# One of a pair's two shifted additions moved from VectorE to a second exponential and an accumulating DMA

## The chip, the cores and the metric

The kernel runs on one core of a Trainium2 chip. The metric is device microseconds of one execution; the kernel is timed in several executions and the median is quoted. A profiled execution gives the rows quoted below. Engines are named as the profile does: PE (TensorE matmul), PEld (its weight load), DVE (VectorE), ACT (ScalarE), POOL (GpSimd), SP (SyncE, which here only issues DMAs).

## What is computed

Two layers of the same "contextual attention" run one after the other over 4 images of 64 channels and 80x80 pixels, so the kernel works through 8 units (layer, image). Cut to what matters, one unit is:

```python
f = b[:, :, ::2, ::2]                       # 40 x 40 positions
w = patches_3x3(f); raw_w = patches_4x4(b, stride 2)
wn = w / max(norm(w), 1e-4)
yi = softmax(10 * (w @ wn.T) * mm, over l) * mm     # 1600 x 1600 scores
patches = yi.T @ raw_w                      # each position's 4x4 patch
out = overlap_add(patches, stride 2) / 4    # pasted back to 80 x 80
```

The overlap-add means that neighbouring scores meet: pasting a 4x4 patch at stride 2 is done here by adding to each score row its neighbour shifted by one position (and by one row of positions), and then multiplying by plain 2x2 blocks of the image.

## The kernel before

Scores lie in SBUF in `G`, 123 partitions (three strips of 41 positions) by 14 tiles. A unit is worked in 4 column chunks (`P_CHUNKS`, 492, 492, 492 and 246 columns) by 7 pairs of tiles: 28 slots a unit. While unit u is pasted, the scores of unit v = u+1 are made, and the features of w = u+2 are prepared. Each engine runs a hand-written program, `body(u, v, w)`, over the 28 slots; the order on each engine is fixed, and semaphores hold the engines together.

For one pair `i` of chunk `k` the softmax and paste steps are, with the slots by which they run ahead of the paste:

- `argument_pair` (DVE, 4 slots ahead, line L923): scales the scores of the pair's two tiles, `arg_tiles(i)` = tiles 2i-1 and 2i, and subtracts the log-sum row held in PSUM (`psB`).
- `softmax_pair` (ACT, 4 slots ahead, L690): one exponential per tile, in place in `G`. On ACT's queue it stands between `copy_scores(j, 0)` and `copy_scores(j, 1)` (L665), which copy or bring score blocks of v from PSUM.
- `shift_pair` (SP, 4 slots ahead, L307): per tile, two DMAs copy the exponentials one partition down and one column on into a buffer of `SH`. The two DMAs are the partition ranges `SHIFT_PARTS`, 112 rows and 10 rows. `SH` has 4 buffers, two pairs' worth.
- `add_shifted` (DVE, 2 slots ahead, L934): `G += SH`, once per tile.
- `sum_pair` (DVE, 1 slot ahead, L952, L953 and L956): adds the tile above and writes `Z`, the weights' moving operand. It waits for the first added tile of the pair that follows, so for the first of the two additions that stand just before it on DVE's queue; the second runs meanwhile.
- `paste_tile` (PE, L504): `Z` times the blocks `B` into `psO`.

Between these, for v, PE makes score blocks (`products`, L454) or takes them by symmetry from stored ones (`transposes`, L463), ACT copies them (L652, L665), DVE combines them (L863) and multiplies and takes the maximum (`score_pair`, L869, L874), and ACT makes the sums of exponentials (`score_sums`, L679). Near the end of a unit the log-sum rows are worked out (`lse_*`, on PE L389), in two parts. SP also lays out the features of the next unit, from `LOHI` into `HL`, `LH`, `H1` and `HV` (`lay_out_features`, L288), loads images (L255), stores results (`store_chunk`, L295) and fetches the strips' border (`shift_strip`, L318, into `SHJ`). GpSimd only runs `wrap` (L1062), a small copy per pair of chunk 0. In the last unit no scores are left to make: the 28 slots hold only argument, exponentials, shifts, sums and paste. Below, "the last unit" is that stretch, from about 1388 us on.

A wait for two semaphores is written as a wait, then `sem_inc` on a gate semaphore, which gives the first wait an instruction to sit on, then the second wait on the operation itself.

Of the kernel before, what the change touches and what calls it, by code (L numbers as in the profile page):

```python
# [5 lines left out]
F32 = mybir.dt.float32  # L6
F16 = mybir.dt.float16
ALU = mybir.AluOpType
ACT = mybir.ActivationFunctionType
# [5 lines left out]
STRIPS, TILES = 3, 14  # L15
PITCH = HALF + 1
TW = STRIPS * PITCH
# [3 lines left out]
GLEN = TW + TILES * TW + WRAP  # L21
PAIRS = TILES // 2
# [7 lines left out]
SLOTS = NK * PAIRS  # L30
NB = NK * TILES
SHIFT_PARTS = [(0, 112), (112, TW - 1)]
STRIP_PARTS = [(0, 80), (80, WRAP)]
BIG = 1.0e30
FREE = 2
SFREE = 4
LSE_FIRST = 4
EXP_AND_LN = 6

# [4 lines left out]
LEAD = 4  # L44
# [36 lines left out]
def contextual_attention(nc, x, mask0, mask1, ident, valid, out):  # L81
    mid = nc.dram_tensor("mid", (IMAGES, C, SIDE, SIDE), F32, kind="Internal").ap()

    with ExitStack() as ctx:
        def sb(name, shape, dt):
            return ctx.enter_context(nc.sbuf_tensor(name, shape, dt))
# [4 lines left out]
        def sem(name):  # L91
            return ctx.enter_context(nc.semaphore(name))

        G = sb("G", [TW, TILES * GLEN], F32)
# [9 lines left out]
        LOHI = sb("LOHI", [128, FLEN], F16)  # L104
        LS, HS = LOHI[0:64, :], LOHI[64:128, :]
        RB = sb("RB", [TW, TILES * TW], F32)
        SH = sb("SH", [TW, SFREE, 4 * TW], F32)
        SHJ = sb("SHJ", [TW, 4 * TW], F32)
        Z = sb("Z", [TW, 2 * FREE, 4 * TW], F32)
        S = sb("S", [TW, 2 * FREE, 4 * TW], F32)  # L110
# [8 lines left out]
        nb = sb("nb", [TW, UNITS * TILES], F32)  # L119
# [61 lines left out]
        act_gate = sem("act_gate")  # L181
        dve_gate = sem("dve_gate")
        pe_gate = sem("pe_gate")
        pool_gate = sem("pool_gate")
# [3 lines left out]
        lse_rows = sem("lse_rows")  # L188
        wrap_made = sem("wrap_made")
        arg_made = sem("arg_made")  # L190
        y_made = sem("y_made")
        sh_in = [sem(f"sh_in{i}") for i in range(SFREE)]
        shj_in = sem("shj_in")
        y1_made = sem("y1_made")
        z_made = sem("z_made")
# [16 lines left out]
        def p_cols(k, wrap=False):  # L212

            s0, n = P_CHUNKS[k]
            return (s0 + 1) * TW, n * TW + (WRAP if wrap and k == NK - 1 else 0)

        def arg_tiles(i):

            return [(2 * i + TILES - 1) % TILES, 2 * i]

        def place(u, v, s):

            unit = u if s < SLOTS else v
            return None if unit is None else (unit, s % SLOTS // PAIRS, s % PAIRS)
# [23 lines left out]
        def _(sp):  # L248
# [49 lines left out]
            def shift_pair(at):  # L298
                u, k, i = at
                c0, n = p_cols(k)  # L300
                for j, t in enumerate(arg_tiles(i)):
                    o = k * TILES + 2 * i + j
                    sp.wait_ge(y_made, u * NB + o + 1)
                    sp.wait_ge(y1_made, u * NB + o + 1)
                    for p0, p1 in SHIFT_PARTS:
                        g = t * GLEN + c0
                        sp.dma_start(SH[p0 + 1:p1 + 1, o % SFREE, 1:n], G[p0:p1, g:g + n - 1]).then_inc(sh_in[o % SFREE], 16)  # L307

            def shift_strip(at):

                u, k, i = at
                c0, n = p_cols(k, True)
                sp.wait_ge(y1_made, u * NB + k * TILES + 1 + SFREE)
                sp.sem_inc(sp_gate, 1)
                sp.wait_ge(z_made, u * SLOTS + k * PAIRS + 1)
                above = (TILES - 1) * GLEN + c0 - TW
                for p0, p1 in STRIP_PARTS:
                    sp.dma_start(SHJ[PITCH + p0:PITCH + p1, 0:n], G[p0:p1, above:above + n]).then_inc(shj_in, 16)  # L318

# [40 lines left out]
            for u in range(UNITS):  # L360
                v, w = (n if n < UNITS else None for n in (u + 1, u + 2))
# [217 lines left out]
        def _(act):  # L579
# [35 lines left out]
            def scale_rows(v, g):  # L615
                act.wait_ge(r_psum, v * 4 + g + 1)
                n = min(4, TILES - 4 * g) * TW
                act.activation(RB[:, 4 * g * TW:4 * g * TW + n], ROW_BANK[g][:, 0:n], ACT.Copy).then_inc(r_rows, 1)

# [63 lines left out]
            def softmax_pair(at):  # L683
                u, k, i = at
                c0, n = p_cols(k)
                for j, t in enumerate(arg_tiles(i)):
                    act.wait_ge(arg_made, u * NB + k * TILES + 2 * i + j + 1)
                    act.sem_inc(act_gate, 1)
                    y = G[:, t * GLEN + c0:t * GLEN + c0 + n]
                    act.activation(y, y, ACT.Exp, bias=nb[:, bass.ds(u * TILES + t, 1)]).then_inc(y_made, 1)  # L690

# [26 lines left out]
            def body(u, v, w):  # L718
                for s in BODY:
# [21 lines left out]
                    if at and not pairs:  # L741
                        softmax_pair(at)
# [4 lines left out]
                    if s == 24 and at:  # L747
                        softmax_pair(at)
# [38 lines left out]
        def _(dve):  # L787
# [7 lines left out]
            dve.sem_inc(z_made, 1)  # L795
            dve.sem_inc(y1_made, SFREE)

# [40 lines left out]
            def score_pair(v, j):  # L838
# [11 lines left out]
                for par, read in enumerate((even_read, odd_read)):  # L850
                    if shared:
# [6 lines left out]
                        if b0:  # L858
# [10 lines left out]
                    dve.tensor_tensor_reduce(S[:, slot + par, 0:n], (odd if par else even)[:, 0:n],  # L869
                                             RB[:, s0 * TW:s0 * TW + n], 1.0, 0.0,  # L870
                                             ALU.mult, ALU.max, mx[:, slot + par:slot + par + 1]).then_inc(max_made, 1)
# [55 lines left out]
            def add_shifted(at):  # L927
                u, k, i = at
                c0, n = p_cols(k)
                for j, t in enumerate(arg_tiles(i)):  # L930
                    o = k * TILES + 2 * i + j
                    dve.wait_ge(sh_in[o % SFREE], (u * (NB // SFREE) + o // SFREE + 1) * 16 * len(SHIFT_PARTS))
                    g = G[:, t * GLEN + c0:t * GLEN + c0 + n]
                    dve.tensor_tensor(g, g, SH[:, o % SFREE, 0:n], ALU.add).then_inc(y1_made, 1)  # L934

            def sum_pair(at, s):
                u, k, i = at
                c0, n = p_cols(k, True)
                slot = 2 * (s % 2)
                dve.wait_ge(y1_made, u * NB + k * TILES + min(2 * i + 3, TILES) + SFREE)  # L940
                dve.sem_inc(dve_gate, 1)
                if k == NK - 1 and i == 0:
                    dve.wait_ge(wrap_made, (u + 1) * PAIRS)
                    dve.sem_inc(dve_gate, 1)
                if i == 0:
                    dve.wait_ge(shj_in, (u * NK + k + 1) * 16 * len(STRIP_PARTS))
                    dve.sem_inc(dve_gate, 1)

                dve.wait_ge(z_used, u * SLOTS + k * PAIRS + i + 1)
                g = G[:, :].rearrange("p (t c) -> p t c", c=GLEN)  # L950
                if i == 0:
                    dve.tensor_tensor(Z[:, slot, 0:n], g[:, 0, c0:c0 + n], SHJ[:, 0:n], ALU.add)  # L952
                    dve.tensor_tensor(Z[:, slot + 1, 0:n], g[:, 1, c0:c0 + n], g[:, 0, c0 - TW:c0 - TW + n],  # L953
                                      ALU.add).then_inc(z_made, 1)
                else:
                    dve.tensor_tensor(Z[:, slot:slot + 2, 0:n], g[:, 2 * i:2 * i + 2, c0:c0 + n],  # L956
                                      g[:, 2 * i - 1:2 * i + 1, c0 - TW:c0 - TW + n], ALU.add).then_inc(z_made, 1)

            def body(u, v, w):
                for s in BODY:  # L960
# [6 lines left out]
                    if at_y:  # L967
                        add_shifted(at_y)
                    at_z = place(u, v, s + 1)
                    if at_z:  # L970
                        sum_pair(at_z, s + 1)
# [56 lines left out]
            for u in range(UNITS):  # L1028
                at = slice(u * TILES, (u + 1) * TILES)
# [15 lines left out]
        @block.gpsimd  # L1045
        def _(pool):
            pool.memset(XP[:, :, :], 0.0).then_inc(xp_cleared, 1)
            pool.memset(SQ[:, :], 0.0).then_inc(cleared, 1)
            pool.memset(LOHI[:, :].bitcast(F32), 0.0).then_inc(cleared, 1)
            pool.wait_ge(cleared, CLEARED)  # L1050
            pool.sem_inc(pool_gate, 1)

            def wrap(u, i):

                if i == 0 and not (isinstance(u, int) and u == 0):
                    pool.wait_ge(z_made, u * SLOTS + 1)
                    pool.sem_inc(pool_gate, 1)
                pool.wait_ge(y1_made, u * NB + 2 * i + 2 + SFREE)
                pool.sem_inc(pool_gate, 1)
                g = G[:, :].rearrange("p (t c) -> p t c", c=GLEN)  # L1060
                g = g[:, 0::TILES - 1, :] if i == 0 else g[:, 2 * i - 1:2 * i + 1, :]
                pool.tensor_copy(g[:, :, GLEN - WRAP:GLEN], g[:, :, TW + PITCH:2 * TW]).then_inc(wrap_made, 1)  # L1062

            def body(u, v):
                for s in BODY:
                    if s < 5 and u is not None:
                        wrap(u, s + 2)
                    if s >= SLOTS and v is not None:
                        wrap(v, 2 * (s - SLOTS))
                        wrap(v, 2 * (s - SLOTS) + 1)  # L1070

            body(None, 0)
            for u in range(UNITS - 1):
                body(u, u + 1)
            body(UNITS - 1, None)


# [20 lines left out]
```

## Time and profile before

| | |
|---|---|
| time, 3 executions | median 1500.39 us (1499.33 to 1503.53) |
| profiled execution, its own time | 1502.71 us |
| its span, first to last instruction | 1500.9 us |
| granted TensorE clock, mean | 0.982 |
| busy | PE 92%, PEld 60%, DVE 81%, ACT 57%, POOL 4% |
| DMA | 149.14 MB, 99 GB/s mean |

A group's row gives busy time, mean length and the idle time just ahead of it on its engine. A window's row gives what each engine was busy in that stretch. A wait's row names the waiting engine and line, what it waited for, total, times and longest. The chain of work that ended last is listed as start, length and what; "issue" is time with no visible releaser, and SPq or DVEq is an engine's queue of non-computing instructions. PE's matmuls are pipelined, and a row that merges several ends with the last one's tail.

### The profile page before, as it was taken

The page shows a single profiled execution, that of the slowest core. Times are in us where ns is not written, and L with a number is a line of the kernel's source. Part 1 is how long each engine was busy: PE and PEld are TensorE (multiplying, and loading weights), DVE is VectorE, ACT ScalarE, POOL GpSimd, SP SyncE. Part 2 cuts the span into 40 slices and gives each one's busy share as a digit, 9 for nine tenths or more (in the row PEclk, how much of TensorE's full clock was granted, in tenths as well). Part 3 has the DMA queues.
Part 4 walks back from the last instruction along what each step waited for, and adds up shares of the span by engine and source line. Part 5 has one row for each costly group of instructions (what it writes and reads, how often), then busy time and mean ns, then how long its engine had stood idle before and what let it go on. Part 6 is the DMA issues. An engine that isn't in the chain of part 4 may idle for free.

```text
span 1500.9 us, 24213 instructions
## 1 busy us (share of the span) xinstructions
PE 1377.1 (92%) x7190; PEld 897.6 (60%) x7190; DVE 1220.5 (81%) x2831; ACT 859.8 (57%) x2233; POOL 54.8 (4%) x63
## 2 busy tenths in 40 slices
PE   4987999989999899998999899998999989999886
PEld 4765665656556565566656576566665656557333
DVE  4668889788888888888898878978888888888984
ACT  2667546666458565584555755666645755457431
POOL 1001000010000100001000000001000010000100
PEclk9998999999999999999999999999999999999999
DMA  5305462254622754136631556215462254523442
GB/s 100 45 1 136 104 124 77 55 154 110 126 68 69 167 107 107 53 98 149 126 88 42 134 119 132 81 50 142 106 135 71 62 149 102 114 58 89 124 137 64
DMA packets 181621, 149.14 MB, mean 99 GB/s; under 512 B 119986, under 2 KB 177394, under 8 KB 181490
## 3 DMA queue, kind: packets, MB, share of 16 engines
q1 hardware_dynamic: 181170, 146.60, 41.1%
q10 hardware_dynamic: 320, 0.99, 0.3%
q8 instruction: 57, 0.93, 0.3%
q14 instruction: 74, 0.61, 0.1%
HBM read 19.76 MB, written 13.11 MB: 22 GB/s over the span
## 4 chain that ended last, share of the span: by engine, by line
PE 39%; DVE 23%; SPq 13%; ACT 9%; issue 8%; DMA 7%; DVEq 0%; POOL 0%; ACTq 0%; POOLq 0%
PE psO L504 18%; PE psG L454 17%; DVE G L923 5%; SPq L307 5%; DVE Z L956 4%; DVE G L863 4%; DVE S L869 3%; SPq L288 3%; DVE G L934 3%; PE psG L463 3%; ACT S L679 3%; DMA HV<-LOHI 3%; SPq L255 3%; DMA SH<-G 2%; ACT G L690 2%
## 5 line engine op out<-in xcount | busy, mean ns | idle before, releaser
L504 PE MATMUL psO<-Z,B 123*128 123x492 f32 (+1 forms) x1792 | 760.9, 553 | 31.3 <-DVE Z L956 19.4
L504 PEld LDWEIGHTS psO<-Z,B 123*128 123x128 f32 x1792 | 324.4, 194 | 260.4 <-issue 180.5
L454 PE MATMUL psG<-LH,HL 128*123 128x246 f16 (+2 forms) x2616 | 408.6, 286 | 24.6 <-DMA HV<-LOHI 19.0
L454 PEld LDWEIGHTS psG<-LH,HL 128*123 128x123 f16 x2616 | 278.0, 138 | 157.9 <-issue 104.5
L869 DVE CUSTOM_DVE_ANT_0 S<-G,RB 123x492 f32<-123x492 f32 (+1 forms) x448 | 268.7, 606 | 86.7 <-DVE G L863 52.1
L690 ACT ACTIVATE G<-G,nb 123x492 f32<-123x492 f32 (+1 forms) x448 | 270.5, 649 | 97.7 <-DVE G L923 97.2
L679 ACT ACTIVATE S<-S,nm 123x480 f32<-123x480 f32 (+3 forms) x560 | 306.9, 554 | 3.5 <-DVE nm L874 3.3
L934 DVE TENSOR_TENSOR G<-G,SH 123x492 f32<-123x492 f32 (+1 forms) x448 | 251.7, 600 | 45.1 <-DMA SH<-G 44.4
L923 DVE SCALAR_TENSOR_TENSOR G<-G,RA,psB 123x492 f32<-123x492 f32 (+1 forms) x448 | 274.8, 656 | 0.3 <-issue 0.3
L665 ACT ACTIVATE G<-psG 123x492 f32<-123x492 f32 (+3 forms) x256 | 120.4, 473 | 189.8 <-PE psG L454 108.3
L956 DVE TENSOR_TENSOR Z<-G 123x984 f32<-123x984 f32 (+1 forms) x192 | 209.1, 1090 | 0.0
L863 DVE TENSOR_TENSOR G<-G,psG 123x492 f32<-123x492 f32 (+2 forms) x272 | 134.1, 493 | 78.4 <-ACT G L665 44.3
L652 ACT ACTIVATE G<-psG 123x246 f32<-123x246 f32 (+1 forms) x136 | 64.2, 472 | 232.8 <-PE psG L454 232.4
L454 PE MATMUL psG<-H 128*123 128x123 f16 (+3 forms) x872 | 194.7, 285 | 0.0
L463 PEld LDWEIGHTS psG<-idn,G 123*123 123x123 f32 x672 | 98.3, 196 | 70.3 <-ACT G L665 23.8
L463 PE MATMUL psG<-idn,G 123*123 123x123 f32 x672 | 113.4, 290 | 24.6 <-ACT G L665 15.2
L454 PEld LDWEIGHTS psG<-H 128*123 128x123 f16 x872 | 103.2, 137 | 20.9
L454 PE MATMUL psG<-HL 128*123 128x492 f16 (+2 forms) x392 | 112.2, 286 | 0.0
L679 ACT ACTIVATION_READ_ACCUMULATOR S<-S,nm 123x1 f32 x560 | 108.1, 193 | 0.0
L1062 POOL COPY G<-G 123x164 f32<-123x164 f32 x56 | 49.9, 892 | 1353.1 <-DVE Z L956 989.6
L699 ACT ACTIVATE OSB<-psO 128x492 f32<-128x492 f32 (+1 forms) x64 | 33.2, 576 | 72.3 <-PE psO L504 72.2
L454 PE MATMUL psG<-HV 128*123 128x246 f16 (+2 forms) x240 | 68.1, 284 | 0.0
(84 smaller groups left out, 580.4 us busy)
## 6 DMA issues: line engine op xcount, KB each, us to landing
SH<-G SPq DMA_DIRECT2D x336, 214.8 KB
SH<-G SPq DMA_DIRECT2D x112, 107.2 KB
SH<-G SPq DMA_DIRECT2D x336, 19.2 KB
XP<-x SPq DMA_DIRECT2D x20, 280.0 KB, 6.2
XP<-mid SPq DMA_DIRECT2D x20, 280.0 KB, 5.7
mid<-OSB SPq DMA_DIRECT2D x52, 80.0 KB, 2.3
out<-OSB SPq DMA_DIRECT2D x52, 80.0 KB, 2.3
HL<-LOHI SPq DMA_DIRECT2D x16, 246.5 KB, 3.5
```

What stands on the lines that cost most here:

```text
L307: sp.dma_start(SH[p0 + 1:p1 + 1, o % SFREE, 1:n], G[p0:p1, g:g + n - 1]).then_inc(sh_in[o % SFREE], 16)
L454: last = pe.matmul(psG[0:TW, bank, b0 * TW:b1 * TW], st[:, p:p + TW], mv[:, lo:lo + n], start=i == 0, stop=i == len(terms) - 1)
L463: last = pe.transpose(psG[0:TW, par, i * TW:(i + 1) * TW], G[:, c:c + TW], idn[0:TW, 0:TW])
L504: last = pe.matmul(psO[:, b, 0:n], B[:, o:o + 128], Z[:, 2 * (s % 2) + j, 0:n], start=t == 0, stop=t == TILES - 1)
L665: act.activation(G[:, c:c + n], psG[0:TW, par, 0:n], ACT.Copy).then_inc(part if shared else read, 1)
L679: last = act.activation(y, y, ACT.Exp, bias=nm[:, k * TILES + t:k * TILES + t + 1], accum_out=sg[:, c:c + 1])
L690: act.activation(y, y, ACT.Exp, bias=nb[:, bass.ds(u * TILES + t, 1)]).then_inc(y_made, 1)
L863: dve.tensor_tensor((odd if par else even)[:, b0 * TW:n], rows[:, p0 * TW:p0 * TW + n - b0 * TW], psG[0:TW, par, b0 * TW:n], ALU.add).then ...
L869: dve.tensor_tensor_reduce(S[:, slot + par, 0:n], (odd if par else even)[:, 0:n], RB[:, s0 * TW:s0 * TW + n], 1.0, 0.0, ALU.mult, ALU.max, ...
L923: dve.scalar_tensor_tensor(out=g, in0=g, scalar=RA[:, bass.ds(u * TILES + t, 1)], in1=psB[0:TW, k % 2, 0:n], op0=ALU.mult, op1=ALU.subtrac ...
L934: dve.tensor_tensor(g, g, SH[:, o % SFREE, 0:n], ALU.add).then_inc(y1_made, 1)
L956: dve.tensor_tensor(Z[:, slot:slot + 2, 0:n], g[:, 2 * i:2 * i + 2, c0:c0 + n], g[:, 2 * i - 1:2 * i + 1, c0 - TW:c0 - TW + n], ALU.add).t ...
```

## The change

For each pair, only the first tile, 2i-1, still goes through `SH` and DVE's addition. For the second tile, 2i, ACT makes the exponential twice: first into a buffer of a new tile `Y`, then, after the first tile's exponential, in place in `G`. GpSimd then issues one DMA that reads `Y`, shifted by one partition and one column, and adds it to `G` (122 rows of up to 491 f32, `accum_op`). `SH` and `Y` have two buffers each, one per pair. `softmax_pair` waits before writing `Y` until the accumulating DMA of the pair two before has landed, and for both arguments of its own pair (`arg_made >= 2*o + 2`) ahead of its first exponential. `sum_pair` and `wrap` wait for their pair's accumulating DMA as well. `sum_pair` still waits for the first tile of the pair that follows, which is now the only addition of that pair. On GpSimd's queue the new `add_copy` stands ahead of `wrap` in each slot.

```diff
-SFREE = 4
+SFREE = 2
...
         SH = sb("SH", [TW, SFREE, 4 * TW], F32)
+        Y = sb("Y", [TW, SFREE, 4 * TW], F32)
...
+        def y1_done(u, k, i):
+
+            n = u * SLOTS + k * PAIRS + i
+            return y1_in[n % SFREE], (n // SFREE + 1) * 16
...
             def shift_pair(at):
                 u, k, i = at
                 c0, n = p_cols(k)
-                for j, t in enumerate(arg_tiles(i)):
-                    o = k * TILES + 2 * i + j
-                    sp.wait_ge(y_made, u * NB + o + 1)
-                    sp.wait_ge(y1_made, u * NB + o + 1)
-                    for p0, p1 in SHIFT_PARTS:
-                        g = t * GLEN + c0
-                        sp.dma_start(SH[p0 + 1:p1 + 1, o % SFREE, 1:n], G[p0:p1, g:g + n - 1]).then_inc(sh_in[o % SFREE], 16)
+                o = u * SLOTS + k * PAIRS + i
+                g = arg_tiles(i)[0] * GLEN + c0
+                sp.wait_ge(y_made, 2 * o + 1)
+                sp.wait_ge(y1_made, o + 1)
+                for p0, p1 in SHIFT_PARTS:
+                    sp.dma_start(SH[p0 + 1:p1 + 1, o % SFREE, 1:n], G[p0:p1, g:g + n - 1]).then_inc(sh_in[o % SFREE], 16)
...
             def softmax_pair(at):
                 u, k, i = at
                 c0, n = p_cols(k)
+                o = u * SLOTS + k * PAIRS + i
+                t = arg_tiles(i)[1]
+                if o >= SFREE:
+
+                    act.wait_ge(*y1_done(u, k, i - SFREE))
+                    act.sem_inc(act_gate, 1)
+                act.wait_ge(arg_made, 2 * o + 2)
+                act.activation(Y[:, o % SFREE, 0:n], G[:, t * GLEN + c0:t * GLEN + c0 + n], ACT.Exp,
+                               bias=nb[:, bass.ds(u * TILES + t, 1)]).then_inc(y_copied, 1)
                 for j, t in enumerate(arg_tiles(i)):
-                    act.wait_ge(arg_made, u * NB + k * TILES + 2 * i + j + 1)
-                    act.sem_inc(act_gate, 1)
+                    if j == 1:
+                        act.wait_ge(y_copied, o + 1)
                     y = G[:, t * GLEN + c0:t * GLEN + c0 + n]
                     act.activation(y, y, ACT.Exp, bias=nb[:, bass.ds(u * TILES + t, 1)]).then_inc(y_made, 1)
...
             def add_shifted(at):
                 u, k, i = at
                 c0, n = p_cols(k)
-                for j, t in enumerate(arg_tiles(i)):
-                    o = k * TILES + 2 * i + j
-                    dve.wait_ge(sh_in[o % SFREE], (u * (NB // SFREE) + o // SFREE + 1) * 16 * len(SHIFT_PARTS))
-                    g = G[:, t * GLEN + c0:t * GLEN + c0 + n]
-                    dve.tensor_tensor(g, g, SH[:, o % SFREE, 0:n], ALU.add).then_inc(y1_made, 1)
+                o = u * SLOTS + k * PAIRS + i
+                t = arg_tiles(i)[0]
+                dve.wait_ge(sh_in[o % SFREE], (o // SFREE + 1) * 16 * len(SHIFT_PARTS))
+                g = G[:, t * GLEN + c0:t * GLEN + c0 + n]
+                dve.tensor_tensor(g, g, SH[:, o % SFREE, 0:n], ALU.add).then_inc(y1_made, 1)

             def sum_pair(at, s):
...
-                dve.wait_ge(y1_made, u * NB + k * TILES + min(2 * i + 3, TILES) + SFREE)
+                dve.wait_ge(y1_made, u * SLOTS + k * PAIRS + min(i + 2, PAIRS) + SFREE)
+                dve.sem_inc(dve_gate, 1)
+                dve.wait_ge(*y1_done(u, k, i))
                 dve.sem_inc(dve_gate, 1)
...
-                pool.wait_ge(y1_made, u * NB + 2 * i + 2 + SFREE)
+                pool.wait_ge(y1_made, u * SLOTS + i + 1 + SFREE)
+                pool.sem_inc(pool_gate, 1)
+                pool.wait_ge(*y1_done(u, 0, i))
                 pool.sem_inc(pool_gate, 1)
...
+            def add_copy(at):
+                u, k, i = at
+                c0, n = p_cols(k)
+                o = u * SLOTS + k * PAIRS + i
+                g = arg_tiles(i)[1] * GLEN + c0
+                pool.wait_ge(y_made, 2 * o + 2)
+                pool.dma_start(G[1:TW, g + 1:g + n], Y[0:TW - 1, o % SFREE, 0:n - 1],
+                               accum_op=ALU.add).then_inc(y1_in[o % SFREE], 16)
+
             def body(u, v):
                 for s in BODY:
+                    at = place(u, v, s + LEAD)
+                    if at:
+                        add_copy(at)
                     if s < 5 and u is not None:
                         wrap(u, s + 2)
```

## Rows read from the trace of the kernel before

**Rows 1.** Page: busy us, share of the span and instructions per engine.
```profile
PE 1377.1 (92%) x7190; PEld 897.6 (60%) x7190; DVE 1220.5 (81%) x2831; ACT 859.8 (57%) x2233; POOL 54.8 (4%) x63
```

**Rows 2.** Windows: one unit, then the last unit (columns: length, PE, PEld, DVE, ACT, POOL, clock).
```profile
720.00:900.00 180.00, 170.28 (x897) 111.49 (x897) 150.34 (x349) 106.83 (x279) 6.22 (x7) 0.98 0.43 104
...
1388.00:1501.00 113.00, 91.70 (x234) 42.56 (x232) 84.18 (x141) 36.91 (x73) 5.57 (x5) 0.98 0.39 108
```

**Rows 3.** Waits of PE, whole span: total us, times, longest.
```profile
PE psO L504 <- DVE Z L956: 19.4, 12, 4.6
PE psG L454 <- DMA HV<-LOHI: 19.0, 7, 3.8
PE psB L389 <- DVE lse L913: 16.6, 8, 2.3
PE psG L463 <- ACT G L665: 15.2, 33, 0.9
PE psO L504 <- DVE Z L953: 9.8, 7, 2.3
```

**Rows 4.** Groups of instructions: the additions and the exponentials.
```profile
L934 DVE TENSOR_TENSOR G<-G,SH 123x492 f32<-123x492 f32 (+1 forms) x448 | 251.7, 600 | 45.1 <-DMA SH<-G 44.4
...
L690 ACT ACTIVATE G<-G,nb 123x492 f32<-123x492 f32 (+1 forms) x448 | 270.5, 649 | 97.7 <-DVE G L923 97.2
```

**Rows 5.** Timeline of one slot of the last unit, and ScalarE's next.
```profile
1444.85 1.36 DVE L923 SCALAR_TENSOR_TENSOR G<-G,RA,psB 123x492 f32<-123x492 f32 x2
1444.99 17.46 PE L504 MATMUL psO<-Z,B 123*128 123x492 f32 x40 [2.20 <-DVE Z L953]
1445.69 1.34 ACT L690 ACTIVATE G<-G,nb 123x492 f32<-123x492 f32 x2 [1.77 <-DVE G L923]
1446.13 1.24 DVE L934 TENSOR_TENSOR G<-G,SH 123x492 f32<-123x492 f32 x2
1447.29 1.18 DVE L956 TENSOR_TENSOR Z<-G 123x984 f32<-123x984 f32 x1
1448.38 1.36 DVE L923 SCALAR_TENSOR_TENSOR G<-G,RA,psB 123x492 f32<-123x492 f32 x2
```

**Rows 6.** Waits of VectorE on itself: a dependent operation behind one gate.
```profile
DVE S L869 <- DVE G L863: 52.1, 276, 0.5
```

**Rows 7.** Chain that ended last, two gates one behind the other on VectorE's queue.
```profile
767.49 0.02 DVEq L857
...
767.64 0.02 DVEq L866
```

**Rows 8.** Timeline of SP and ScalarE where one unit gives way to the next.
```profile
668.88 2.79 SPq L307 DMA_DIRECT2D SH<-G  x4
671.87 1.16 SPq L288 DMA_DIRECT2D HL<-LOHI  x2
...
679.21 1.35 ACT L690 ACTIVATE G<-G,nb 123x492 f32<-123x492 f32 x2 [0.76 <-DVE G L923]
...
685.84 1.29 ACT L690 ACTIVATE G<-G,nb 123x492 f32<-123x492 f32 x2
```

**Rows 9.** Timeline where score blocks begin to be taken by transposing stored ones.
```profile
778.59 1.35 DVE L923 SCALAR_TENSOR_TENSOR G<-G,RA,psB 123x492 f32<-123x492 f32 x2
779.43 1.34 ACT L690 ACTIVATE G<-G,nb 123x492 f32<-123x492 f32 x2 [0.45 <-DVE G L923]
...
781.29 0.69 PE L463 MATMUL psG<-idn,G 123*123 123x123 f32 x4 [0.85 <-ACT G L665]
```

**Rows 10.** Chain that ended last: from a shift's last issue to its landing.
```profile
742.58 5.26 DMA SH<-G
...
1485.59 1.95 DMA SH<-G
```

**Rows 11.** SP's issues of the shifts, all of them: ns min/median/max.
```profile
L307 SPq DMA_DIRECT2D SH<-G x896: 517/759/2252, 119.9 to 1485.6; - x180
```

**Rows 12.** DMA queue of SP: packets, MB, share of 16 engines.
```profile
q1 hardware_dynamic: 181170, 146.60, 41.1%
```

More of the change, by code:

```diff
@@ L190, in contextual_attention @@
         arg_made = sem("arg_made")
+        y_copied = sem("y_copied")
         y_made = sem("y_made")
         sh_in = [sem(f"sh_in{i}") for i in range(SFREE)]
+        y1_in = [sem(f"y1_in{i}") for i in range(SFREE)]
         shj_in = sem("shj_in")
@@ L312, in shift_strip @@
                 c0, n = p_cols(k, True)
-                sp.wait_ge(y1_made, u * NB + k * TILES + 1 + SFREE)
+                sp.wait_ge(y1_made, u * SLOTS + k * PAIRS + 1 + SFREE)
                 sp.sem_inc(sp_gate, 1)
```

## The prediction

> **What bounds the kernel now.** I read the page's busy shares first: PE 92%, DVE 81%, ACT 57%, POOL 4% [rows 1]. The reader is to see that VectorE, which the change relieves, is not the busiest. A share is a mean over stages, so I went on to windows. One unit is 180 us, and PE is busy in 170.3 of it [rows 2]: at most 9.7 us a unit can come back if every wait of PE goes, whatever VectorE gains. In the last unit, where no scores are left to make, PE has 91.7 of 113 us and VectorE 84.2 [rows 2]: there the two alternate.
>
> The waits of PE then say what its holes wait for. VectorE's sums `Z` account for 19.4 + 9.8 = 29.2 us in the whole span, the laid-out features (`HV`) for 19.0, the log-sum row for 16.6, ScalarE's score copies for 15.2 [rows 3]. So 29.2 us is what relief of VectorE can directly return, and two of the other three holes hang on ScalarE and on the DMAs, to which the change gives work.
>
> **The change part by part.**
>
> *VectorE loses 224 additions.* There are 448 at 600 ns [rows 4], so 224 x 0.600 = 134 us of busy time. That is not time off the queue. Before, `sum_pair` waits for the first of two additions, and the second hides that wait: additions begin at 1446.13 and `Z` begins at 1447.29, 1.16 us later [rows 5]. After, the addition just ahead of `Z` is the very one that it waits for. One addition lasts about 1.24 - 0.58 = 0.66 us (two in 1.24, `Z` following 0.58 after the second began) [rows 5]. A dependent operation behind one gate starts 52.1/276 = 0.19 us after its releaser [rows 6], and the new wait for the accumulating DMA adds a second gate, 767.64 - 767.49 = 0.15 us [rows 7]. So `Z` would start 0.66 + 0.19 + 0.15 = 1.00 us after the addition begins, and a wide slot gains 0.16 us, not 0.58. A pair at a chunk's end doesn't have this exposed wait, which I leave as a reserve. Bounds: nothing gained (gates 0.16 longer) to 0.58 a slot (gates hidden).
>
> What is this worth? Within the units PE covers it. In the last unit VectorE's slot is 1448.38 - 1444.85 = 3.53 us, and PE's is about 17.46/5 = 3.49 (40 matmul records, 8 a slot) [rows 5]; 21 wide slots can gain 0.04 to 0.08 each, 1 to 2 us. There is a second relief: SP issues two DMAs a pair fewer, 759 ns each at the median [rows 11], so 1.5 us a pair. VectorE's additions wait 44.4 us for the shifts altogether [rows 4], mostly hidden behind PE; in the last unit I take one such 1.5 us back for each of three or four chunks. I book VectorE and SP together at -6 us, with 0 and -29 as bounds.
>
> *ScalarE gets 224 exponentials more.* 224 x 0.649 = 145 us [rows 4], 860 [rows 1] to 1005 us busy, 67%. Mostly it waits for PE, and this is hidden. Two places are not. Where score blocks begin to be transposed, PE waits for ScalarE's copy [rows 9]. Before, the exponentials begin at 779.43, during the second argument; after, the first of three must wait for that argument's end, 778.59 + 1.35 = 779.94, and lasts one exponential more, about 0.63 us. Together that is 0.5 + 0.65 + the restart, up to 1.3 us, against VectorE arriving up to 1 us earlier because the shifts land sooner. I take +0.8 in each of 7 units: +5.5 (bounds 0 and +9). Ahead of the log-sum row ScalarE works without gaps, and PE waits 16.6 us for that row in 8 units [rows 3]; two half-wide exponentials more in front of it, each under 0.649 us, I take at 0.4: 8 x 0.8 = +6.5 (bounds 0 and +10).
>
> *GpSimd's accumulating DMA.* No such transfer is in this trace. What counts is its latency L from the end of the pair's third exponential to its landing, because ScalarE may write `Y` again only two pairs later; behind that wait on ScalarE's queue stand the score copies on which PE waits. Bounds from the nearest rows: SP issues a shift in 0.52 to 2.25 us [rows 11], and from the last issue to the landing it is 1.95 us alone and 5.26 us behind other transfers [rows 10]. So 2.5 to 7.5 us, if adding costs what copying costs and a software issue what SP's does. I take about 5 alone and 6.5 beside other transfers, nearer the upper end, since a third access is made for each element.
>
> The cover in the last unit: arguments end at 1444.85 + 1.36 = 1446.21, three exponentials take some 2.0 us more (two in 1.34 [rows 5]), ending near 1448.25; the `Y` after next is due two slots after 1446.28, at 1453.34. Cover 5.1 us, so L = 5 just fits: 0. In a unit's slots of about 6.4 us (180/28) the cover is 2 x 6.4 - 2.0 = 10.8. At a unit's end it is short: exponentials end at 679.21 + 1.35 = 680.56 and the pair after next begins at 685.84 [rows 8], already two pairs apart with one between, 5.3 us before and less after the third exponential; the feature loads fill the DMA engines then. I take 1.5 us of stall a unit: +10 for 7. SP reaches the first feature DMA one or two shift issues sooner (four in 2.79 us [rows 8]), about 0.9 us, x7 = -6; but the accumulating transfers now run beside the features instead of queueing behind them on SP, which I price at as much, +6. `wrap`, behind `add_copy` on GpSimd's queue, has two slots to spare: 0.
>
> A rule prices this transfer lower. The Trainium skill ("DMA: Bandwidth & Descriptors", section "Anatomy of one DMA — SWDGE (gpsimd) path") puts a DMA issued by GpSimd at 2.0 us plus bytes over 436 GB/s; for 122 x 1964 bytes that is 2.6 us, an estimate from that page. By it the +10 and the last unit's stall would fall away, and the sum would be about 0. It has no price for the addition, and no row here shows the transfer.
>
> **Sum.** -6 + 5.5 + 6.5 + 10 - 6 + 6 = +16, from which I take 5 us for overlap, since a stall of ScalarE and the late log-sum row fall into the same unit change: +11. The profiled execution's own time is 1502.7, 1.8 over its span; the median is 1500.4, 2.3 below. 1500.4 + 11 = 1511 us.
>
> **Rivals.**
>
> *A wash or a small gain* (the other side). L stays under 5 us everywhere, so ScalarE never stalls, and `Z` waits less for shifts. It decides if L < 5.1 us alone and the exposed wait ahead of `Z` is under 0.34 us. For it: PE waits 29.2 us on `Z` [rows 3], and half of that, with 1.5 us a chunk on SP, would be -20: 1481. Against it: PE hides most of VectorE's time. The milder form, terms that cancel, gives 1496 to 1505.
>
> *L about 7.5 us.* Both upper bounds at once. Slot length in the last unit becomes (7.5 + 2.0)/2 = 4.7 us: 21 x 1.2, plus 7 narrow slots with some 2.4 more, is +42, and the unit changes another 2.2 x 7 = +15: 1568.
>
> *The transfer runs on two engines.* 122 rows, unlike 112, share no factor above 2 with 16. SP's queue moved 146.6 MB in 41.1% of 16 engines' span [rows 12], 14.9 GB/s an engine, so a row of 1964 bytes takes 0.132 us, and 61 rows on one engine 8.1 us. With 2 to 3 us around it L is 10 to 11, the whole cover of an ordinary slot: the last unit loses 21 x 2.7 + 7 x 4, about 85, the unit changes 5 x 7 = 35, short slots some 40: about 1670; if adding doubles a row's time, ScalarE paces every slot and it is 2000 or more. For it: `SHIFT_PARTS` is split at 112. Against it: the split concerns SP's issue, not GpSimd's.
>
> The Trainium skill (the same page, section "Why a DMA increments its semaphore by 16 and not by 1") says that the number of engines is the largest up to 16 that divides both sides' slowest dimension, which gives 2 for 122, and then that GpSimd gives some direct copies all 16 engines. No run here shows which holds when adding.
>
> *The change does not do what it says* (VectorE isn't relieved because `Z` waits in place of the second addition): part of my forecast, no case of its own.
>
> **How the numbers follow.** About 0.3% (4.5 us) is what a measurement of this kernel can tell from no change. Forecast (1503 to 1530): 0.33. L long: 0.15. Two engines: 0.15. Wash: 0.17. Gain: 0.20. Faster: 0.22, the gain and 0.02 of the wash; same 0.18, the rest of the wash and 0.03 at the forecast's lower edge; slower 0.60, what is left. The range must leave out no more than 2 in 10: from 1482, the gain's price, to 1600, beyond which lie the two-engine case's times; most of the 2 in 10 is there. The forecast's own range is 1503 to 1530.
>
> **What would show it.** Right: VectorE's busy time some 130 us lower but its idle time ahead of L956 and its successors up by 0.3 us a slot; ScalarE near 1005 us; PE's idle time longer at L389 and at the transposes; ScalarE idle ahead of the `Y` exponential, released by a DMA, mainly at the units' ends. Wrong: no idle time of ScalarE on that DMA (L short: the gain), or such idle time in every slot (L over 10.8: two engines). I would be most wrong on L, for which this trace has only neighbours.

## The result and the profile after

The changed kernel takes 1586.53 us (median of 4 runs, 1582.53 to 1600.04) against 1501.32 us before (4 runs, 1499.33 to 1503.53): a ratio of 1.0574, with a 95% interval of 1.0533 to 1.0615. It is slower, as forecast, but by 85 us where 11 were forecast.

First the page after: the span, the engines [rows 1] and the DMA queues [rows 12].

```profile
span 1580.7 us, 23819 instructions
...
PE 1397.5 (88%) x7190; PEld 909.6 (58%) x7190; DVE 1122.6 (71%) x2607; ACT 973.0 (62%) x2457; POOL 211.4 (13%) x287
...
q1 hardware_dynamic: 148018, 99.63, 28.4%
q0 software_dynamic: 32256, 46.97, 24.6%
```

VectorE lost 98 us of busy time and ScalarE gained 113; the prediction had 134 and 145. PE does the same 7190 matmuls in 20 us more; its mean granted clock went from 0.982 to 0.964. On the queues the reader is to compare the two lines: GpSimd's queue (q0) moves less than half of SP's bytes, and its packets take nearly as much of the engines' time. Per engine and per time that its packets took, an accumulating transfer moves 46.97 MB / (0.246 x 16 x 1580.7 us) = 7.5 GB/s, where SP's queue moved 14.9 before [rows 12].

The waits of PE and of VectorE, and two of ScalarE (columns as in [rows 3]):

```profile
PE psG L463 <- DMA HV<-LOHI: 37.6, 7, 7.4
PE psO L513 <- DVE Z L976: 24.5, 13, 3.8
PE psG L472 <- ACT G L674: 23.7, 39, 1.8
PE psG L463 <- DVE G L881: 20.4, 7, 3.8
PE psB L398 <- DVE lse L931: 17.4, 8, 2.7
PE psO L513 <- DVE Z L973: 16.2, 10, 2.9
```
```profile
DVE G L952 <- DMA SH<-G: 107.7, 20, 8.4
...
DVE Z L976 <- DVE G L952: 27.1, 105, 0.3
DVE Z L976 <- DMA G<-Y: 12.8, 47, 0.6
```
```profile
ACT Y L702 <- DVE G L941: 115.7, 63, 6.7
...
ACT Y L702 <- DMA G<-Y: 10.7, 5, 2.9
```

PE's wait for the laid-out features doubled (19.0 to 37.6 [rows 3]), the one for `Z` grew by 11.5, that for ScalarE's copies by 8.5, and that for VectorE's additions that make up score blocks (L881) from 8.4 by the same view of before to 20.4. VectorE waits 107.7 us for half as many shifts, against 44.4 [rows 4], in only 20 waits, so over 5 us each. The 27.1 us of `Z` on the addition are the exposed wait that the prediction speaks of. The two waits that the change itself adds, of `Z` and of ScalarE on the accumulating DMA, are small, 12.8 and 10.7 us, and they are not on PE's list.

So the place to look at is where shifts land late. The timeline of SP, GpSimd and VectorE after, then the chain that ended last, where images are loaded:

```profile
770.41 0.84 POOL L1092 DMA_DIRECT2D G<-Y  x1 [5.04 <-ACT G L708]
...
770.72 8.91 SPq L265 DMA_DIRECT2D XP<-mid  x6
...
776.24 0.84 POOL L1092 DMA_DIRECT2D G<-Y  x1 [4.99 <-ACT G L708]
...
788.15 0.67 DVE L952 TENSOR_TENSOR G<-G,SH 123x492 f32<-123x492 f32 x1 [7.83 <-DMA SH<-G]
```
```profile
777.81 1.82 SPq L265
779.73 1.09 SPq L316
780.87 7.26 DMA SH<-G
788.15 0.68 DVE G L952
```

Six image loads took SP 6.48 us to issue before (by the same view) and take 8.91 now, with two accumulating transfers started beside them. All 36 issues of such loads (columns as in [rows 11]):

```profile
L265 SPq DMA_DIRECT2D XP<-mid x36: 602/1364/2175, 538.6 to 1348.2; - x36
```

The median was 664 ns in the same view of before. The shift that stands behind them in SP's queue lands 7.26 us after its last issue, against 5.26 [rows 10], and VectorE stands still for 7.83 us. Before, at the same place, it waited 4.26 us for the pair's first shift and 0.21 for the second:

```profile
746.98 0.67 DVE L934 TENSOR_TENSOR G<-G,SH 123x492 f32<-123x492 f32 x1 [4.26 <-DMA SH<-G]
747.87 0.67 DVE L934 TENSOR_TENSOR G<-G,SH 123x492 f32<-123x492 f32 x1 [0.21 <-DMA SH<-G]
```

Two windows of 6 us, first before and then after, show what PE makes of it (columns as in [rows 2]; the last three are granted clock, DMA share and GB/s):

```profile
741.00:747.00 6.00, 6.00 (x47) 4.49 (x46) 1.70 (x6) 2.75 (x6) 0.00 (x0) 1.00 1.21 217
747.00:753.00 6.00, 5.72 (x23) 2.93 (x22) 5.38 (x13) 1.69 (x6) 0.00 (x0) 1.00 0.37 110
```

```profile
782.00:788.00 6.00, 5.33 (x36) 3.19 (x34) 0.00 (x0) 3.40 (x8) 0.84 (x1) 1.00 1.19 180
788.00:794.00 6.00, 3.35 (x7) 1.87 (x8) 5.18 (x13) 0.00 (x0) 0.00 (x0) 0.72 0.21 54
```

In the first window after, VectorE does nothing, and PE goes on with work whose inputs are there. The packets' times add up to more than the window on all 16 engines (a share of 1.19), as they did before (1.21), but they move 180 GB/s where it was 217. In the second PE runs out and is busy for 3.35 of 6 us, where it was 5.72; with that its granted clock falls from the upper level (1.00, 2.4 GHz) to a mean of 0.72, part of it at 1.2 GHz.

Where units change, SP's queue shows the same:

```profile
703.71 2.80 SPq L298 DMA_DIRECT2D HL<-LOHI  x2
...
710.04 2.47 SPq L298 DMA_DIRECT2D HV<-LOHI  x2
```

Here `HL` takes 2.80 us to issue instead of 1.16 [rows 8], and the landing of `HV` took 8.32 us by the chain, 5.60 before. From the third layout of features to the last, five units on, it is 1277.07 - 326.78 = 950.3 us, against 1211.92 - 314.54 = 897.4 before: 10.6 us a unit.

### The profile page after: what moved, and what is told of

Its sections match the earlier page's. It is cut to its first block, busy times and chain, and to the rows that moved or that the text cites. A ratio compares the mean times of both kernels' runs of the same rounds, so it can differ in the third digit from the quotient of the medians.

```text
span 1580.7 us, 23819 instructions
## 1 busy us (share of the span) xinstructions
PE 1397.5 (88%) x7190; PEld 909.6 (58%) x7190; DVE 1122.6 (71%) x2607; ACT 973.0 (62%) x2457; POOL 211.4 (13%) x287
## 3 DMA queue, kind: packets, MB, share of 16 engines
q0 software_dynamic: 32256, 46.97, 24.6%
## 4 chain that ended last, share of the span: by engine, by line
PE 41%; DVE 14%; ACT 12%; SPq 12%; DMA 12%; issue 8%; DVEq 0%; POOL 0%; ACTq 0%; POOLq 0%
PE psO L513 19%; PE psG L463 18%; DVE G L941 4%; SPq L298 4%; DMA HV<-LOHI 3%; SPq L265 3%; DMA SH<-G 3%; ACT G L708 3%; ACT Y L702 3%; ACT S L688 3%; DVE G L881 3%; SPq L316 2%; DMA SHJ<-G 2%; SPq L305 2%; ACT G L674 2%
## 5 line engine op out<-in xcount | busy, mean ns | idle before, releaser
L513 PE MATMUL psO<-Z,B 123*128 123x492 f32 (+1 forms) x1792 | 773.9, 562 | 42.1 <-DVE Z L976 24.5
L513 PEld LDWEIGHTS psO<-Z,B 123*128 123x128 f32 x1792 | 330.6, 197 | 277.1 <-issue 187.2
L463 PE MATMUL psG<-LH,HL 128*123 128x246 f16 (+2 forms) x2616 | 414.5, 288 | 62.3 <-DMA HV<-LOHI 37.6
L1092 POOL DMA_DIRECT2D G<-Y x224 | 188.6, 842 | 1353.0 <-ACT G L708 1326.8
L708 ACT ACTIVATE G<-G,nb 123x492 f32<-123x492 f32 (+1 forms) x448 | 266.0, 643 | 0.0
L976 DVE TENSOR_TENSOR Z<-G 123x984 f32<-123x984 f32 (+1 forms) x192 | 210.6, 1097 | 44.0 <-DVE G L952 27.1
L702 ACT ACTIVATE Y<-G,nb 123x492 f32<-123x492 f32 (+1 forms) x224 | 145.7, 650 | 127.3 <-DVE G L941 115.7
L952 DVE TENSOR_TENSOR G<-G,SH 123x492 f32<-123x492 f32 (+1 forms) x224 | 134.9, 602 | 107.7 <-DMA SH<-G 107.7
L881 DVE TENSOR_TENSOR G<-G,psG 123x492 f32<-123x492 f32 (+2 forms) x272 | 134.4, 494 | 91.3 <-ACT G L674 47.8
```

The source lines that it names most:

```text
L463: last = pe.matmul(psG[0:TW, bank, b0 * TW:b1 * TW], st[:, p:p + TW], mv[:, lo:lo + n], start=i == 0, stop=i == len(terms) - 1)
L513: last = pe.matmul(psO[:, b, 0:n], B[:, o:o + 128], Z[:, 2 * (s % 2) + j, 0:n], start=t == 0, stop=t == TILES - 1)
L702: act.activation(Y[:, o % SFREE, 0:n], G[:, t * GLEN + c0:t * GLEN + c0 + n], ACT.Exp, bias=nb[:, bass.ds(u * TILES + t, 1)]).then_inc(y_c ...
L881: dve.tensor_tensor((odd if par else even)[:, b0 * TW:n], rows[:, p0 * TW:p0 * TW + n - b0 * TW], psG[0:TW, par, b0 * TW:n], ALU.add).then ...
L1092: pool.dma_start(G[1:TW, g + 1:g + n], Y[0:TW - 1, o % SFREE, 0:n - 1], accum_op=ALU.add).then_inc(y1_in[o % SFREE], 16)
```

## The experiments

The theory after this reading: the accumulating transfers hold up SP's transfers, above all where features or images are loaded. Against it stood the third exponential, the new waits, and a fault in the booked relief. Every ratio is to the kernel before, with its 95% interval. The kernels that leave out an addition, or part of it, serve the timing alone.

**The relief alone.** The after kernel without the third exponential, the accumulating DMA and the waits for it.

```
-                act.wait_ge(*y1_done(u, k, i - SFREE))
-                act.activation(Y[:, ...], G[...], ACT.Exp, ...).then_inc(y_copied, 1)
...
-                        add_copy(at)
```

> The changed kernel without the exponential into Y and without the accumulating DMA: the second tile gets no shifted addition at all. VectorE and SP are relieved as the change intends, at no price; the exposed wait and both gates ahead of the sums stay. Theory 1 or 2: at or below before, 1480 to 1502, and this is the most that the relief can give. Theory 3: 1550 or more.

Measured: 1472.62 us, 0.981 (0.979 to 0.9829), below the range expected. The relief is worth 28.8 us, the far bound of the -29 to 0 in the prediction. Which half of it, VectorE's addition or SP's two issues? Three kernels take these apart.

The before kernel without the second tile's shift, while VectorE makes both additions:

```
-                    for p0, p1 in SHIFT_PARTS:
+                    for p0, p1 in SHIFT_PARTS if j == 0 else []:
```

> The kernel before, without the second tile's two shift DMAs; VectorE still makes both additions, the second with the first tile's buffer, so the second tile's result is another. If the half kernel's 29 us come from SP's and the DMA engines' relief: 1473 to 1482. If they come from VectorE's: 1496 to 1503.

Measured: 1473.5 us, 0.9815 (0.9801 to 0.983). VectorE does all of its old work, and the whole gain is there. So 28 of the 28.8 us are the shift's. Taking VectorE's addition away, with the exposed wait and the two gates that come in its place, is worth about 1 us, too little to tell from none. VectorE's waits for the shift in this kernel:

```profile
DVE G L937 <- DMA SH<-G: 18.4, 8, 3.2
```

The before kernel with four issues a pair, of which one carries 16 rows instead of 112:

```
+                    for p0, p1 in SHIFT_PARTS if j == 0 else [(0, 16), SHIFT_PARTS[1]]:
```

> The kernel before with all four shift issues a pair, but the second tile's larger one cut from 112 rows to 16 (it leaves the second tile's other rows without their right shifted addition). If the half kernel's gain was SP's issue time: 1496 to 1503. If it was the transferred bytes: 1474 to 1485.

Measured: 1499.68 us, 0.9982 (0.9963 to 1.0001), no change that can be told. A quarter of SP's bytes went (146.6 to 109.66 MB) and nothing came back, so it isn't the bytes that gave the gain.

Two things are left: SP's two issues, and VectorE's wait for the second shift to land, which went with them. The timelines speak for the issues. At the image load of the same unit VectorE waits as follows in the kernel with few bytes, and in the one with one shift:

```profile
746.95 1.25 DVE L934 TENSOR_TENSOR G<-G,SH 123x492 f32<-123x492 f32 x2 [4.82 <-DMA SH<-G]
```
```profile
734.23 1.25 DVE L937 TENSOR_TENSOR G<-G,SH 123x492 f32<-123x492 f32 x2 [2.66 <-DMA SH<-G]
```

With few bytes the wait for the second shift is gone there (the two additions follow one another, in one row), and yet the kernel is no faster. What shrinks with the issues is the wait for the first shift, which SP reaches sooner.

The before kernel with both tiles' shifts in one DMA for each range of partitions, two issues a pair and all of the bytes. It leaves nothing out:

```
-                    for p0, p1 in SHIFT_PARTS:
-                        g = t * GLEN + c0
-                        sp.dma_start(SH[p0 + 1:p1 + 1, o % SFREE, 1:n], G[p0:p1, g:g + n - 1])...
+                for p0, p1 in SHIFT_PARTS:
+                    sp.dma_start(SH[p0 + 1:p1 + 1, o % SFREE:o % SFREE + 2, 1:n], g[p0:p1, :, c0:c0 + n - 1])...
```

> The kernel before, complete, with the shifts of a pair's two tiles carried by one DMA for each partition range: two issues a pair on SP instead of four, for the same bytes; the first tile's shift then starts only when both exponentials are made. If the half kernel's gain was SP's issue time: 1475 to 1485. If it was the transferred bytes: 1497 to 1505, or a little above for the later start.

Measured: 1489.08 us, 0.9927 (0.991 to 0.9945), between the two ranges expected. This is the fastest version found that leaves nothing out, 12 us under the kernel before. SP's issues of the shifts [rows 11], PE's wait for features [rows 3] and VectorE's for shifts:

```profile
L307 SPq DMA_DIRECT2D SH<-G x448: 602/812/2567, 120.9 to 1468.3; - x150
```
```profile
DVE G L937 <- DMA SH<-G: 45.3, 18, 4.6
...
PE psG L455 <- DMA HV<-LOHI: 9.5, 6, 2.8
```

Half as many issues at 812 ns instead of 759, and features that PE waits for half as long. It keeps less than half of the relief: VectorE waits for shifts as long as before (45.3 us, where one shift a pair left 18.4), as the pair's first addition now needs both exponentials and a larger transfer. Which of these two holds it up was not taken apart.

**The transfer, in steps.** The after kernel with everything as it is, but 16 rows in the accumulating DMA:

```
-                pool.dma_start(G[1:TW, g + 1:g + n], Y[0:TW - 1, o % SFREE, 0:n - 1],
+                pool.dma_start(G[1:17, g + 1:g + n], Y[0:16, o % SFREE, 0:n - 1],
```

> The changed kernel, with the accumulating DMA cut from 122 rows to 16; everything else stays, ScalarE's third exponential and all waits too. It leaves out the addition in the other 106 rows. Theory 1 (the accumulating transfers load the 16 DMA engines beside the feature and image loads, and PE waits for what these bring): most of the 85 us goes, 1495 to 1520 us, with PE's wait for HV near the 19 us of before and the features' last landing near 5.6 us instead of 8.3. Theory 2 (ScalarE's third exponential and its later start delay the score copies): 1570 to 1590. Theory 3 (the exposed wait ahead of the sums on VectorE): 1570 to 1590.

Measured: 1499.33 us, 0.999 (0.9979 to 1.0002). All 85 us are gone, with the third exponential, the waits and 224 DMAs in place. PE's wait for features is at 20.7 us again, VectorE's for shifts at 33.3:

```profile
DVE G L952 <- DMA SH<-G: 33.3, 16, 3.8
...
PE psG L463 <- DMA HV<-LOHI: 20.7, 7, 3.6
```

Then the whole transfer, but copying into a scratch tile instead of adding:

```
+                pool.dma_start(W[1:TW, o % SFREE, 1:n], Y[0:TW - 1, o % SFREE, 0:n - 1]).then_inc(y1_in[o % SFREE], 16)
```

> The changed kernel, with GpSimd's DMA of the same 122 rows as a plain copy into a scratch tile: it leaves out the addition of the second tile's shifted copy. Theory 1 in the form that adding takes about twice the engine time of a copy (the trace after: 7.5 GB/s an engine against 14): about half of the loss goes, 1530 to 1555. Theory 1 in the form that it is only the place, beside the loads and no longer behind them in SP's queue: 1570 to 1590. Theories 2 and 3: 1570 to 1590.

Measured: 1525.9 us, 1.0162 (1.0139 to 1.0185), below both ranges expected. GpSimd's queue in this kernel:

```profile
q0 software_dynamic: 13440, 46.97, 11.5%
```

The packets of the same bytes take 11.5% of the 16 engines' span instead of 24.6%, and there are 60 of them a transfer instead of 144: 46.97 MB / (0.115 x 16 x 1519.8 us) = 16.8 GB/s an engine, 2.2 times the rate of adding. Copying 122 rows costs 1525.9 - 1499.3 = 26.6 us more than adding 16. Adding 122 rows instead of copying them costs 60.6 more; the copy goes to another tile, so what the destination does is in this number too.

**The third exponential.** The after kernel without it (`Y` holds zeros), and the same with 16 rows:

> The changed kernel without the exponential into Y (Y is zero, so nothing is added for the second tile); the DMA, its size and all waits stay, among them ScalarE's for both arguments. Theory 1: 1565 to 1590. Theory 2: 1500 to 1530.

Measured: 1549.21 us, 1.0319 (1.0281 to 1.0357), between the ranges of both theories: each holds in part.

> The changed kernel without the exponential into Y and with the accumulating DMA cut to 16 rows; all waits stay. It leaves out the second tile's shifted addition. If the 27 us between the half kernel (1473) and the 16-row kernel (1499) are ScalarE's third exponential: 1472 to 1480. If they are the waits on the DMA, or the small DMA itself: 1492 to 1500.

Measured: 1476.57 us, 0.9841 (0.9808 to 0.9873). So the exponential costs 1499.3 - 1476.6 = 22.8 us where the transfer is small and 1586.5 - 1549.2 = 37.3 where it is whole: it is not free, and it adds to a delay that is already there. PE's waits at the transposes without it are 15.8 us, with it 22.6, both at 16 rows:

```profile
PE psG L472 <- ACT G L674: 15.8, 38, 1.2
```
```profile
PE psG L472 <- ACT G L674: 22.6, 40, 1.3
```

**Where it costs.** The after kernel, in which ten of a unit's 28 slots, those about the image and feature loads, send 16 rows and the others all:

```
+                rows = 17 if k * PAIRS + i in (3, 4, 5, 6, 7, 8, 12, 13, 14, 15) else TW
```

> The changed kernel, with the accumulating DMA cut to 16 rows in those 10 of a unit's 28 slots in which features are laid out or images loaded (slots 3 to 8 and 12 to 15 of the pair's own count); 122 rows in the other 18. It leaves out the addition in 106 rows there. If the loss arises where these loads are late: 1500 to 1520. If it arises evenly in all slots: 1499 + 87 x 18/28 = about 1555.

Measured: 1501.86 us, 1.0007 (0.9993 to 1.0022). GpSimd's queue still moves 30.32 of 46.97 MB by adding, and that costs 1501.9 - 1499.3 = 2.5 us, too little to tell from none. If all slots lost alike, 1555 us were expected. No kernel cut ten other slots, so that the place matters, and not only the amount, rests on this run beside the timelines above.

And the opposite: the before kernel, complete, to which GpSimd adds the same 224 accumulating transfers, of zeros into a scratch tile that nobody reads.

```
+                pool.dma_start(W[1:TW, o % 2, 1:n], Y[0:TW - 1, o % 2, 0:n - 1],
+                               accum_op=ALU.add).then_inc(y1_in[o % 2], 16)
```

> The kernel before, complete, with the accumulating DMAs as an extra load: GpSimd adds 122 rows of zeros to a scratch tile for each pair at the time at which the change does it. Nobody but GpSimd waits for them; ScalarE, VectorE and SP do what they did before. If the load on the DMA engines is enough by itself: 1550 to 1600. If it needs the change's other parts (the third exponential, the waits on its landing): 1500 to 1525.

Measured: 1616.73 us, 1.0765 (1.071 to 1.0821), above the range expected: 115 us for transfers on which no engine but GpSimd waits. VectorE's wait for the shifts, and PE's for features (44.4 [rows 4] and 19.0 [rows 3] before):

```profile
DVE G L937 <- DMA SH<-G: 141.0, 47, 9.5
```
```profile
PE psG L457 <- DMA HV<-LOHI: 37.3, 7, 7.0
```

**Another way.** The second addition goes to GpSimd as an operation of its own, with no accumulating DMA and no third exponential:

```
+                pool.tensor_tensor(g, g, SH[:, o % SFREE, 0:n], ALU.add).then_inc(y2_made, 1)
```

> The kernel before, complete, with the second addition of each pair made by GpSimd's own tensor addition instead of VectorE's; SP's four shift DMAs a pair and ScalarE's two exponentials as before. If the 29 us that the half kernel gained come from VectorE's relief: 1475 to 1490. If they come from SP's and the DMA engines' relief: 1498 to 1505. If GpSimd's addition slows VectorE or is late for the sums: 1510 or more.

Measured: 1531.34 us, 1.0198 (1.0179 to 1.0216), slower than before and faster than the change. GpSimd's additions and VectorE's:

```profile
L1079 POOL TENSOR_TENSOR G<-G,SH 123x492 f32<-123x492 f32 (+1 forms) x224 | 255.4, 1141 | 1228.8 <-DMA SH<-G 1199.6 <-DVE G L938 28.8
...
L962 DVE TENSOR_TENSOR Z<-G 123x984 f32<-123x984 f32 (+1 forms) x192 | 230.0, 1198 | 44.1 <-DVE G L938 41.0 <-PE psO L508 2.4 <-POOL G L1079 0.7
...
L938 DVE TENSOR_TENSOR G<-G,SH 123x492 f32<-123x492 f32 (+1 forms) x224 | 149.0, 665 | 41.0 <-DMA SH<-G 40.9
```

SP keeps its four issues here, so the relief that counts is missing. VectorE's own operations are longer beside GpSimd's: the addition has a mean of 665 ns instead of 600 [rows 4], `Z` of 1198 instead of 1097 in the after kernel. Whether this makes all of the 30 us is not shown.

## Why the prediction was right in sign and wrong in size

The medians make one sum: relief -28.8 (relief alone); the new waits, ScalarE's for both arguments among them, and the 16-row transfers +3.9 (1476.6 - 1472.6); third exponential +22.8; copying 122 rows +26.6; adding instead of copying +60.6. Together +85.1. The order in which parts are put back shifts costs between the terms, as the exponential's 22.8 and 37.3 show.

That the sign came out right was in part luck. With the relief at its measured size in place of the booked one, and the other terms as they stood, the prediction's sum would have been a small gain: -28.8 + 5.5 + 6.5 + 10 - 6 + 6 = -6.8, and less with the 5 for overlap. Two errors, a relief booked at a fifth of its size and a load on the DMAs that was taken as free, went opposite ways. The measured time is far outside the forecast's own 1503 to 1530; the wider range, to 1600, holds it only by the part above that, where the prediction had put a long L, which did not occur. None of the rivals had the mechanism that the runs showed.

**VectorE and SP, -6 (bounds 0 and -29): -28.8.** That VectorE's 224 additions are worth next to nothing was right: both additions stay in the kernel with one shift, and the time is the relief's. The size was wrong on SP's side. I counted 1.5 us back for a few chunks of the last unit alone and called the shifts hidden behind PE elsewhere. SP's issue time is in every unit ahead of features and shifts; fewer bytes gave nothing, fewer issues for the same bytes gave 12 us.

**The exposed wait ahead of `Z`.** Right. The timeline of the last unit after:

```profile
1502.59 1.36 DVE L941 SCALAR_TENSOR_TENSOR G<-G,RA,psB 123x492 f32<-123x492 f32 x2
1503.87 0.67 DVE L952 TENSOR_TENSOR G<-G,SH 123x492 f32<-123x492 f32 x1
1504.79 1.18 DVE L976 TENSOR_TENSOR Z<-G 123x984 f32<-123x984 f32 x1 [0.26 <-PE psO L513]
1505.89 1.36 DVE L941 SCALAR_TENSOR_TENSOR G<-G,RA,psB 123x492 f32<-123x492 f32 x2
```

From addition to `Z` it is 0.92 us, forecast 1.00, 1.16 before [rows 5]; two gates cost 0.26, forecast 0.34. The slot is 3.30 us against 3.53, so where nothing is late a slot did get faster. The last unit as a whole did not: from PE's last matmul for the image blocks (L435, L444 after) to the end it is 1580.7 - 1462.4 = 118.3 us, against 1500.9 - 1386.4 = 114.5, where 1 to 2 us less were forecast. SP stores results there (L295, L305 after), six transfers that take 6.38 us to issue instead of 3.97, and the shift behind them keeps VectorE waiting for 4.89 us. So features and images are not the only transfers that are held up, but 76 of the 80 us between the profiled spans lie ahead of this unit.

**ScalarE, +5.5 and +6.5: +22.8.** The place at the transposes was right: PE waits there 15.8 us without the exponential and 22.6 with it. The log-sum row was not: that wait is 17.4 in both. Between the two kernels with 16 rows, PE's waits grew by 6.8 us at the transposes, by 3.7 for the features (17.0 to 20.7) and by 7.3 for `Z` (9.0 to 16.3, both lines): 17.8 of the 22.8. I had looked for ScalarE's delay at two places; it also reached `Z` and the features, presumably by the shifts, which wait for exponentials at the head of SP's queue (SP's waits for ScalarE's exponentials grew from 244.2 to 335.2 us, while those for VectorE's additions fell from 567.3 to 510.5).

**ScalarE's stall on the transfer, +10.** The total is near (five waits, 10.7 us) and the place is wrong. I booked 1.5 us at each unit's end and none in the last unit; one wait of 1.7 us lies in the units and four are in the last unit. ScalarE's next exponentials before, and its waits on the transfer from 1470 us on after:

```profile
692.70 1.29 ACT L690 ACTIVATE G<-G,nb 123x492 f32<-123x492 f32 x2
```
```profile
ACT Y L702 <- DMA G<-Y: 9.1, 4, 2.9
```

The prediction misread [rows 8]: the exponentials at 679.21 and 685.84 belong to neighbouring pairs, and the pair after next begins at 692.70. So the cover at a unit's end was 692.70 - 680.56 = 12.1 us, less the third exponential, and not 5.3, and by it nothing was to be booked there. In the last unit, where L = 5 was to fit in 5.1, it did not always. No run tells what these 9.1 us cost. L itself was about right:

```profile
DMA to landing us min/median/max: 3.0/4.4/8.5
```

I had taken 5, and 6.5 under load. This row refutes the two-engine rival, which needs over 8.1 us in each slot and a kernel near 1670. The rival of a long L, whose 1568 us are nearest to the measured time, is not borne out either: its price was ScalarE's stall in every slot of the last unit and at every unit's end. The Trainium skill's formula ("DMA: Bandwidth & Descriptors", section "Anatomy of one DMA — SWDGE (gpsimd) path"), 2.6 us as the prediction worked it out, is below the 3.0 of the least landing measured.

**SP sooner, -6, against contention, +6: the step that failed most.** I let these two cancel: what leaves SP's queue runs beside it, "which I price at as much". It was priced by the bytes, which are the same, and not by the time that their packets take, which is 2.2 times as much when adding. And a transfer on SP's queue waits its turn, while one from GpSimd starts as soon as its exponentials are made (0.3 us after, at 770.41), beside the loads on which PE and VectorE wait next. The whole transfers instead of 16 rows, copying and adding together, are +87.2. The theory is borne out from both sides: the load alone makes the kernel before 115 us slower, and thinning it in ten of 28 slots gives all 85 us back. What the transfers contend for, the 16 engines or another part of their path, no run tells.

The loss does not need slower issues on SP. In the loaded kernel before, which loses more, SP's issue of the image loads stays near its old 664 ns:

```profile
L258 SPq DMA_DIRECT2D XP<-mid x36: 602/700/2561, 549.2 to 1364.2; - x36
```

There late landings go with the loss: from issue to landing an image load took 6.1 us at the median before, 6.9 in this kernel and 7.1 in the changed one, and VectorE waits 141.0 us for shifts. SP's issue of image loads is slow in the changed kernel (1364 ns) and in the one without the third exponential (1136), both of which add 122 rows into `G`; it is 700 where the same rows are added or copied into a scratch tile. Why, and how much of the 85 us it makes, is open. A version that keeps the accumulating transfer in 18 slots and the old path in ten was not tried; the thinned kernel (1501.9 us), which in those ten leaves out 106 rows of the addition, does not suggest a gain over the kernel before.

## What to carry to other kernels

Moving an addition into an accumulating DMA doesn't make it free: price it by a measured rate for adding, and look at whose loads are in flight at that moment. An engine's busy share said nothing here (VectorE at 81% gave back about 1 us for 98); the queue that only issues was worth 28. When a queue's issues are the limit, try to carry more in each transfer before moving work to another queue: here that gave 12 us.

## What the runs showed that was not expected

An accumulating DMA from GpSimd moved 7.5 GB/s an engine in 144 packets, a plain copy of the same shape 16.8 in 60. An issue can be dear where its bytes are not: with the second tile's shift cut from 112 rows to 16 in its large part the time was 1499.7 us, with that shift gone 1473.5.
